# The tanh rows of an additive-attention kernel in a ring of 10240 columns in place of eight buffers, with half the descriptor scratch

## Chip, cores and metric

The program runs on one core of a Trainium2 chip. The metric is the device time of one execution in microseconds (us); the time before is the median of three runs. The profile is one execution of the same program, recorded instruction by instruction.

## The reference, cut to what matters

Eight images of 56x56 positions with 128 channels go through two layers. The first is a deformable convolution with an MLP. The second is causal additive attention over the S = 3136 positions of an image, then an expert layer that picks eight tokens for each of 64 experts. The change touches the attention scores alone:

```python
f = jnp.einsum('bih,ha->bia', x, W1[:h])
g = jnp.einsum('bjh,ha->bja', x, W1[h:])
t = jnp.tanh(f[:, :, None, :] + g[:, None, :, :] + b1)
scores = jnp.einsum('bija,a->bij', t, w2[:, 0]) + b2[0]
e = jnp.exp(scores) * flag
```

For each pair of a query i and an earlier key j there are A = 16 tanh values, which are weighted and summed to one score.

## The kernel before, in words

**Blocks, chunks, units, groups.** The positions of an image are cut into NBLK = 25 blocks of 128 queries (the last has 64). Block k attends to the key tiles 0 to k. `chunks_of(k)` cuts these k + 1 tiles into the fewest equal chunks of at most CHUNK = 1024 keys, so a chunk is 128 to 1024 columns wide. A *unit* is one ScalarE instruction: the tanh of eight queries times 16 values (128 partitions) against the keys of a chunk (`what == "unit"`, L1678). A full chunk has 16 units, and PLACES = 4 *groups* of four units (two in the last block). TensorE reduces a group with `score_w` into a bank pair of PSUM (`what == "score"`, L1846); `score_ps` holds two chunks. When all four groups of a chunk are scored, ScalarE takes the exponential (`what == "exp"`, L1688), and TensorE and VectorE turn it and multiply it with the values. An image has 800 units, 208 groups and 52 chunks.

**The tanh buffers.** `tanh` is `[128, TANH_SLOTS, CHUNK]`, eight buffers of 1024 columns. Unit `ui` writes the first w columns of buffer `ui % 8`. Before that it waits on the semaphore `scored` until the group of unit `ui - 8` has been scored.

**The other work.** The same engines run the convolution (`image_in`, `conv`, `offsets`, `weights`), the chain of each block (`turn`, `mix`, `hidden`, `mlp_out`, `keys`) and the sampling. For the sampling GpSimd (POOL) issues the gathers: one `sample` step is SAMPLES = 18 indirect DMAs (L1189), each fetching 128 rows of 512 bytes into one of GATHER_SLOTS = 4 buffers. VectorE multiplies and sums a buffer (L1373, L1376), and that frees it: POOL waits on `sampled` for it. There are NSUB = 49 sample steps for an image, 392 in all, and two of them feed a block's chain, whose end (`keys`, L1418 to L1421) the first unit of the block waits for (`keys_copied`).

**The order of work.** Each engine runs its steps in one fixed order, with no choice at run time. The order comes from a planner in the kernel: `needs()` lists what each step waits for, `due_times()` gives priorities and `simulate()` lays the steps out by the costs in `LASTS` and `lasts()`. The period so found is repeated for each image by a loop (`walk`); the first and last images have orders of their own. In the order that the planner gives for the kernel before, ScalarE has its `exp` of a chunk 0 to 4 units behind the last unit of the chunk in 44 of the 52 chunks, and between 6 and 24 units behind in the other eight. In that plan POOL is busy without a pause, and the wait for the tanh buffers is what starts 23 of the 800 units.

**After the last image**, parts of `tanh` hold the last image's routing scores (`tanh_flat`, `score7`, `chosen7`, `chosenT7`), 8064 columns in all.

**Descriptor scratch.** The program is built with the default of 16384 bytes per partition, kept for the descriptors of the DMAs that POOL issues.

Of the kernel before, what the change touches and what calls it, by code (L numbers as in the profile page):

```python
# [8 lines left out]
ACT = mybir.ActivationFunctionType  # L9
# [3 lines left out]
P = 128  # L13
# [18 lines left out]
CHUNK = 1024  # L32
# [4 lines left out]
GATHER_SLOTS = 4  # L37
PIECE = 3
X1_SLOTS = 10
TANH_SLOTS = 8  # L40
PLACES = 4
FLOOR_MAGIC = 8388608.0
RSQRT_MAGIC = 1597463007.0 - 2.0 ** 30 - 2.0 ** 22
# [10 lines left out]
def chunks_of(k):  # L54

    tiles = k + 1
    n = -(-tiles * P // CHUNK)
    cuts = [tiles * i // n for i in range(n + 1)]
    return [list(range(cuts[i], cuts[i + 1])) for i in range(n)]


def chunk_width(tiles):
    return sum(blk_rows(j) for j in tiles)
# [77 lines left out]
def group_of(k, c, s):  # L141

    return k, c, s // (blk_rows(k) // 32)


UNIT_GROUP = [GROUP_INDEX[group_of(*u)] for u in UNIT_INDEX]


SLOT_OF = [0, 1, 2, 3] * 10 + [0, 1, 2] * 3
# [127 lines left out]
def needs():  # L277
# [3 lines left out]
    def at(age, engine, what, *place):  # L281
        return age, engine, (what, *place)
# [64 lines left out]
        out["sp", ("logits", k)] = [at(0, "dve", "logits", k), at(0, "sp", "route", k)]  # L347
    for i, u in enumerate(units):
        ci = CHUNK_INDEX[u[:2]]
        ring = units[i - TANH_SLOTS if i >= TANH_SLOTS or UNITS % TANH_SLOTS == 0 else -1]  # L350
        out["act", ("unit", *u)] = [at(0, "dve", "keys", u[0]), at(int(i < TANH_SLOTS), "pe", "score", *group_of(*ring))]
        if u[2] == group_units(u[0], group_of(*u)[2])[-1]:
            out["pe", ("score", *group_of(*u))] = [at(0, "act", "unit", *u),
                                                   at(int(ci < 2), "act", "exp", *chunks[ci - 2])]
# [335 lines left out]
def network(nc, io, x2_d, xln2_d, logits_d, patches_d, chosen_d, expert_d, out, images):  # L690
    with ExitStack() as ctx:
        def sb(name, shape, dt=F32):
            return ctx.enter_context(nc.sbuf_tensor(name, shape, dt))
# [4 lines left out]
        def sem(name):  # L698
# [64 lines left out]
        key_rep = sb("key_rep", [P, EARLY * P + S])  # L763
        query = sb("query", [P, NBLK * A])
        values = sb("values", [P, NBLK + EARLY, C + 1])
        tanh = sb("tanh", [P, TANH_SLOTS, CHUNK])
        expo = sb("expo", [P, 2, CHUNK])
        expoT = sb("expoT", [P, 2, 4, P])
        den = sb("den", [P, 2])
# [33 lines left out]

        slots = [pool_mem[:, at:at + 2 * PER * HID].rearrange("p (w e h) -> p w e h", w=2, e=PER)
                 for at in SLOTS_AT]
        tanh_flat = tanh[:].rearrange("p a b -> p (a b)")
        score7 = tanh_flat[:E, 0:S]
        chosen7 = tanh_flat[:E, S:2 * S]
        chosenT7 = tanh_flat[:ROW_P, 2 * S:2 * S + ROW_T * E].rearrange("p (t e) -> p t e", e=E)
# [830 lines left out]
        @block.scalar  # L1640
        def _(act):
            for ln in (h_ready, mask_exp, gelu_done, tanh_done, exp_done):
                nc.scalar.sem_inc(ln.sem, ln.lead)
            act.wait_ge(consts_ready, 1)

            def wait(ln, image, i):
                act.wait_ge(ln.sem, ln.after(image, i))

            def task(n, odd, name):
                what, i = (*name, 0)[:2]  # L1650
                if what == "conv":
                    wait(conv_done, n, i)
                    wait(params_done, n, i - 1)
                    nc.scalar.activation(h_band[:], side_ps[:, :BAND], ACT.Gelu, bias=bn[:, 1:2], scale=bn[:, 0:1])\
                        .then_inc(h_ready.sem, 1)
                elif what == "offsets":
                    wait(mask_shifted, n, i)
                    nc.scalar.activation(mask[:], mask[:], ACT.Exp).then_inc(mask_exp.sem, 1)
                elif what == "hidden":
                    r = blk_rows(i)  # L1660
                    wait(hid_done, n, i)
                    wait(mlp_done, n, i - 1)
                    for c in range(HID // P):
                        last = nc.scalar.activation(hid[:, c, :r], chain_ps[:, c * P:c * P + r], ACT.Gelu,  # L1664
                                                    bias=b_hid[:, c:c + 1])
                    last.then_inc(gelu_done.sem, 1)
                elif what == "unit":
                    k, c, s = name[1:]
                    ui = UNIT_INDEX[k, c, s]
                    if (c, s) == (0, 0):  # L1670
                        wait(keys_copied, n, k)

                    wait(scored, n, UNIT_GROUP[ui - TANH_SLOTS] - (GROUPS_SCORED if ui < TANH_SLOTS else 0))
                    tiles = chunks_of(k)[c]
                    w = chunk_width(tiles)
                    lo = key_column(odd, tiles[-1] if odd else tiles[0])
                    col = k * A + row_group(k, s)
                    nc.scalar.activation(tanh[:, ui % TANH_SLOTS, :w], key_rep[:, lo:lo + w], ACT.Tanh,  # L1678
                                         bias=query[:, col:col + 1]).then_inc(tanh_done.sem, 1)
                elif what == "exp":  # L1680
                    k, c = name[1:]
                    r = blk_rows(k)
                    ci = CHUNK_INDEX[k, c]
                    w = chunk_width(chunks_of(k)[c])
                    wait(scored, n, GROUP_INDEX[k, c, PLACES - 1])

                    wait(exp_turned, n, last_quad_of_chunk(ci - 2))
                    nc.scalar.activation(expo[:r, ci % 2, :w], score_ps[:r, ci % 2, :w], ACT.Exp, bias=tiny[:r, 2:3])\  # L1688
                        .then_inc(exp_done.sem, 1)

                elif what == "u_exp":
                    r = E * len(units[i])
                    act.wait_ge(differ_ready, i + 1)
                    nc.scalar.activation(score[:r], score[:r], ACT.Exp, bias=neg[:r], accum_out=total[:r, 0:1])
                    nc.scalar.drain().then_inc(prob_ready, 1)
                elif what == "e_gelu":
                    act.wait_ge(e_biased, STEPS)
                    nc.scalar.activation(pre, pre, ACT.Gelu).then_inc(e_act, 1)
                elif what == "l_exp":
                    act.wait_ge(last_top, 1)  # L1700
                    nc.scalar.activation(score7, score7, ACT.Exp, bias=neg[:E], accum_out=total[:E, 0:1])
                    nc.scalar.drain().then_inc(last_prob, 1)
                elif what == "l_gelu":
                    act.wait_ge(last_biased, i + 1)
                    part = pre7[:, :, i * PER:(i + 1) * PER]
                    nc.scalar.activation(part, part, ACT.Gelu).then_inc(last_act, 1)

            walk(act, "act", task)

        @block.tensor  # L1710
        def _(pe):
# [10 lines left out]
            def wait(ln, image, i):  # L1722
                pe.wait_ge(ln.sem, ln.after(image, i))
# [25 lines left out]
            def task(n, odd, name):  # L1749
# [84 lines left out]
                elif what == "score":  # L1834
# [8 lines left out]
                    for lo in range(0, w, 512):  # L1843
                        hi = min(w, lo + 512)
                        for col, ui in enumerate(four):
                            last = mm(score_ps[32 * col:32 * col + 32, ci % 2, lo:hi], score_w[:, place],  # L1846
                                      tanh[:, ui % TANH_SLOTS, lo:hi], start=place == 0, stop=place == PLACES - 1)
                    last.then_inc(scored.sem, 1)
                elif what == "values":
                    k, c, q = name[1:]  # L1850
# [277 lines left out]
```

## Time and profile before

| | us |
|---|---|
| median of 3 runs | 15138.87 |
| lowest, highest | 15132.04, 15160.17 |
| profiled execution | 15154.41 |
| its span, first to last instruction | 15152.6 |
| ScalarE busy | 6766.0 (45%) |
| TensorE matmul busy | 7392.2 (49%) |
| VectorE busy | 6055.5 (40%) |
| POOL busy | 6690.9 (44%) |

A row of a view names the engine, the source line, the operation and its tiles (out<-in), and the idle time before it in square brackets with what ended it. The start of a matmul in the profile is when TensorE takes it up, and its end is modelled. "remote" as what ended a wait means that the semaphore rose at a time at which no instruction was seen to end.

### The profile page before, as it was taken

The page shows a single profiled execution, that of the slowest core. Times are in us where ns is not written, and L with a number is a line of the kernel's source. Part 1 is how long each engine was busy: PE and PEld are TensorE (multiplying, and loading weights), DVE is VectorE, ACT ScalarE, POOL GpSimd, SP SyncE. Part 2 cuts the span into 40 slices and gives each one's busy share as a digit, 9 for nine tenths or more (in the row PEclk, how much of TensorE's full clock was granted, in tenths as well). Part 3 has the DMA queues.
Part 4 walks back from the last instruction along what each step waited for, and adds up shares of the span by engine and source line. Part 5 has one row for each costly group of instructions (what it writes and reads, how often), then busy time and mean ns, then how long its engine had stood idle before and what let it go on. Part 6 is the DMA issues. An engine that isn't in the chain of part 4 may idle for free.

```text
span 15152.6 us, 152058 instructions
## 1 busy us (share of the span) xinstructions
PE 7392.2 (49%) x45113; PEld 3712.8 (25%) x45113; DVE 6055.5 (40%) x17780; ACT 6766.0 (45%) x8210; POOL 6690.9 (44%) x7060
## 2 busy tenths in 40 slices
PE   3345553445534555345444455444554445544557
PEld 1222222222222222122222222222222222222234
DVE  4443334433443334344344433434334434354343
ACT  1245642455424554245533455334553346533454
POOL 4444444444444444444444444444444444444430
PEclk6667776677766777677766677667776677766778
DMA  2111111111111111111111111111111111212325
GB/s 63 52 44 35 34 40 48 43 32 35 42 46 41 32 38 43 45 40 32 39 41 45 39 33 39 42 47 38 33 37 43 48 37 32 58 55 70 95 63 161
DMA packets 453936, 712.02 MB, mean 47 GB/s; under 512 B 146576, under 2 KB 261136, under 8 KB 451472
## 3 DMA queue, kind: packets, MB, share of 16 engines
q0 software_dynamic: 225792, 462.87, 11.6%
q1 hardware_dynamic: 227312, 239.24, 5.0%
q8 instruction: 378, 6.19, 0.2%
q14 instruction: 454, 3.72, 0.1%
HBM read 595.58 MB, written 105.96 MB: 46 GB/s over the span
## 4 chain that ended last, share of the span: by engine, by line
another core or an unknown queue 37%; ACT 20%; PE 13%; issue 12%; DVE 12%; DVEq 5%; DMA 1%; SPq 0%; POOL 0%; ACTq 0%; POOLq 0%
ACT tanh L1678 17%; PE score_ps L1846 6%; DVEq L1208 4%; DVE pool_mem L1373 2%; DVE newton L1242 2%; PE value_ps L1875 2%; DVE rstd L1244 1%; PE side_ps L1778 1%; DVE bst L1249 1%; ACT L1664 1%; PE turn_ps L1747 1%; ACT expo L1688 1%; ACT L1688 1%; ACT hid L1664 1%
## 5 line engine op out<-in xcount | busy, mean ns | idle before, releaser
L1678 ACT ACTIVATE tanh<-key_rep,query 128x896 f32<-128x896 f32 (+7 forms) x6400 | 5557.8, 951 | 5014.7 <-remote 2819.6
L1189 POOL DMA_INDIRECT pool_mem<-patches_odd,pool_mem x3528 | 3346.8, 949 | 4037.8 <-DVE y L1376 3014.6
L1189 POOL DMA_INDIRECT pool_mem<-patches_even,pool_mem x3528 | 3344.0, 948 | 3988.4 <-DVE y L1376 2890.2
L1846 PE MATMUL score_ps<-tanh,score_w 128*32 128x512 f32 (+3 forms) x24320 | 3613.8, 639 | 2235.8 <-ACT tanh L1678 1285.3
L1846 PEld LDWEIGHTS score_ps<-tanh,score_w 128*32 128x32 f32 x24320 | 832.7, 125 | 4411.0 <-issue 2787.7
L1875 PE MATMUL value_ps<-values,expoT 128*128 128x129 f32 (+1 forms) x5200 | 1009.8, 345 | 341.9 <-issue 275.8
L1373 DVE TENSOR_TENSOR pool_mem<-pool_mem 128x384 f32<-128x384 f32 x2352 | 1135.8, 552 | 50.7 <-issue 49.1
L1376 DVE TENSOR_REDUCE y<-pool_mem 128x64 f32<-128x2304 f32 x392 | 1000.8, 2553 | 53.2 <-issue 24.7
L1875 PEld LDWEIGHTS value_ps<-values,expoT 128*128 128x128 f32 (+1 forms) x5200 | 891.6, 248 | 435.4 <-issue 350.3
L1747 PE MATMUL turn_ps<-ident,expo 128*128 128x128 f32 (+1 forms) x2632 | 564.1, 339 | 830.6 <-DVE expoT L1442 433.6
L1442 DVE COPY expoT<-turn_ps 128x512 f32<-128x512 f32 (+4 forms) x800 | 457.1, 572 | 1203.2 <-remote 843.6
L1688 ACT ACTIVATE expo<-score_ps,tiny 128x896 f32<-128x896 f32 (+9 forms) x416 | 383.1, 921 | 831.9 <-remote 666.9
L1688 ACT ACT_TABLE_LOAD x206 | 264.3, 1283 | 883.9 <-remote 697.6
L1747 PEld LDWEIGHTS turn_ps<-ident,expo 128*128 128x128 f32 (+1 forms) x2632 | 381.9, 175 | 1000.1 <-DVE expoT L1442 458.1
L1266 DVE TENSOR_TENSOR biased<-chain_ps,rows 128x128 f32<-128x128 f32 (+1 forms) x400 | 115.3, 288 | 1234.4 <-remote 880.4
L1242 DVE SCALAR_TENSOR_TENSOR newton<-rstd,newton 128x1 f32<-128x1 f32 (+1 forms) x2403 | 529.1, 220 | 193.0 <-issue 14.3
L1815 PE MATMUL chain_ps<-chainT,w_fc 128*128 128x128 f32 (+1 forms) x1600 | 328.0, 371 | 512.3 <-DVE chainT L1395 412.4
L1664 ACT ACTIVATE hid<-chain_ps,b_hid 128x128 f32<-128x128 f32 (+1 forms) x800 | 226.3, 365 | 709.8 <-remote 504.0
L1822 PE MATMUL chain_ps<-w_fc,hid 128*128 128x128 f32 (+1 forms) x1600 | 281.8, 330 | 421.2 <-ACT hid L1664 288.3
L1831 PE MATMUL chain_ps<-chainT,w_key 128*128 128x128 f32 (+1 forms) x400 | 142.6, 457 | 704.6 <-DVE chainT L1411 505.4
L1244 DVE SCALAR_TENSOR_TENSOR rstd<-newton,rstd 128x1 f32<-128x1 f32 (+1 forms) x2403 | 385.1, 160 | 213.3 <-issue 21.9
L1778 PE MATMUL side_ps<-pool_mem,early 128*128 128x448 f32 x1008 | 423.3, 575 | 93.2 <-DVEq L1208 87.5
(166 smaller groups left out, 6210.9 us busy)
## 6 DMA issues: line engine op xcount, KB each, us to landing
pool_mem<-in_weight SPq DMA_DIRECT2D x64, 1024.0 KB, 9.2
pool_mem<-patches_even,pool_mem POOLq DMA_INDIRECT x3528
pool_mem<-patches_odd,pool_mem POOLq DMA_INDIRECT x3528
patches_even<-pool_mem SPq DMA_DIRECT2D x104, 256.0 KB, 2.0
patches_odd<-pool_mem SPq DMA_DIRECT2D x104, 256.0 KB
pool_mem<-in_x SPq DMA_DIRECT2D x56, 224.0 KB
x_tok<-in_x SPq DMA_DIRECT2D x192, 64.0 KB
x_d<-x SPq DMA_DIRECT2D x192, 64.0 KB
```

The source lines that it names most:

```text
L1189: pool.indirect_dma_start(gathered[:, b, j * 4 * CG:(j + 1) * 4 * CG], None, patches_flat[int(odd)], bass.IndirectOffsetOnAxis(ap=index[:, ...
L1208: return v.drain()
L1242: v.scalar_tensor_tensor(newton[:r, 1:2], rstd[:r], rstd[:r], newton[:r, 0:1], ALU.mult, ALU.mult)
L1244: v.scalar_tensor_tensor(rstd[:r], newton[:r, 1:2], 1.5, rstd[:r], ALU.add, ALU.mult)
L1373: v.tensor_tensor(part, part, weight[:, lo:lo + PIECE].unsqueeze(2) .to_broadcast([P, PIECE, CG, 4]), ALU.mult)
L1376: v.tensor_reduce(y[:, i // 2 % 2, b].rearrange("p (g c) -> p g c", c=CG), product.rearrange("p (g t) c k -> p g c t k", g=2), AX_XY, ALU. ...
L1678: nc.scalar.activation(tanh[:, ui % TANH_SLOTS, :w], key_rep[:, lo:lo + w], ACT.Tanh, bias=query[:, col:col + 1]).then_inc(tanh_done.sem, 1)
L1688: nc.scalar.activation(expo[:r, ci % 2, :w], score_ps[:r, ci % 2, :w], ACT.Exp, bias=tiny[:r, 2:3])\
L1747: return mm(out, src, ident[:r, :r], is_transpose=True, start=True, stop=True)
L1778: last = mm(side_ps[:, :BAND], taps[:, t], x_pad[:, i * BAND_ROWS + dy:(i + 1) * BAND_ROWS + dy, dx:dx + W], start=t == 0, stop=t == TAPS - 1)
L1846: last = mm(score_ps[32 * col:32 * col + 32, ci % 2, lo:hi], score_w[:, place], tanh[:, ui % TANH_SLOTS, lo:hi], start=place == 0, stop=pl ...
L1875: last = mm(value_ps[:r, :C + 1], expoT[:wj, pi % 2, z, :r], values[:wj, value_place(odd, j)], start=j == 0, stop=j == k)
```

## The change

The rows of `tanh` are packed: a unit gets w columns of a ring of TANH_COLUMNS = 10240, directly behind the unit before it, or at column 0 where it does not fit before the end. `tanh_before(i)` finds the latest earlier unit whose columns overlap those of unit i, and the wait is for that unit's group. The same rule goes to the planner's `needs()`, so the order of the engines may change. The descriptor scratch is halved to 8192 bytes per partition; the ring takes the 2048 more columns of four bytes that this leaves.

```diff
-TANH_SLOTS = 8
+TANH_COLUMNS = 10240
+def tanh_ring():
+    places, at = [], 0
+    for k, c, s in UNIT_INDEX:
+        w = chunk_width(chunks_of(k)[c])
+        at = 0 if at + w > TANH_COLUMNS else at
+        places.append((at, at + w))
+        at += w
+    return places
+TANH_AT = tanh_ring()
+def tanh_before(i):
+    lo, hi = TANH_AT[i]
+    for j in range(i - 1, i - UNITS - 1, -1):
+        a, b = TANH_AT[j % UNITS]
+        if a < hi and lo < b:
+            return j
+TANH_BEFORE = [tanh_before(i) for i in range(UNITS)]
...
-        ring = units[i - TANH_SLOTS if i >= TANH_SLOTS or UNITS % TANH_SLOTS == 0 else -1]
-        out["act", ("unit", *u)] = [at(0, "dve", "keys", u[0]), at(int(i < TANH_SLOTS), "pe", "score", *group_of(*ring))]
+        ring = TANH_BEFORE[i]
+        out["act", ("unit", *u)] = [at(0, "dve", "keys", u[0]), at(int(ring < 0), "pe", "score", *group_of(*units[ring]))]
...
-        tanh = sb("tanh", [P, TANH_SLOTS, CHUNK])
+        tanh = sb("tanh", [P, TANH_COLUMNS])
...
-                    wait(scored, n, UNIT_GROUP[ui - TANH_SLOTS] - (GROUPS_SCORED if ui < TANH_SLOTS else 0))
+                    old = TANH_BEFORE[ui]
+                    wait(scored, n, UNIT_GROUP[old] - (GROUPS_SCORED if old < 0 else 0))
...
-                    nc.scalar.activation(tanh[:, ui % TANH_SLOTS, :w], key_rep[:, lo:lo + w], ACT.Tanh,
+                    nc.scalar.activation(tanh[:, TANH_AT[ui][0]:TANH_AT[ui][1]], key_rep[:, lo:lo + w], ACT.Tanh,
...
-                                      tanh[:, ui % TANH_SLOTS, lo:hi], start=place == 0, stop=place == PLACES - 1)
+                                      tanh[:, TANH_AT[ui][0] + lo:TANH_AT[ui][0] + hi], start=place == 0, stop=place == PLACES - 1)
...
-    nc = bacc.Bacc("TRN2", target_bir_lowering=False, num_devices=1)
+    nc = bacc.Bacc("TRN2", target_bir_lowering=False, num_devices=1, dynamic_dma_scratch_size=8192)
```

## Rows read from the trace of the kernel before

**Rows 1.** The page: span, busy time, and the chain that ended last.
```profile
span 15152.6 us, 152058 instructions
PE 7392.2 (49%) x45113; PEld 3712.8 (25%) x45113; DVE 6055.5 (40%) x17780; ACT 6766.0 (45%) x8210; POOL 6690.9 (44%) x7060
...
another core or an unknown queue 37%; ACT 20%; PE 13%; issue 12%; DVE 12%; DVEq 5%; DMA 1%; SPq 0%; POOL 0%; ACTq 0%; POOLq 0%
ACT tanh L1678 17%; PE score_ps L1846 6%; DVEq L1208 4%; DVE pool_mem L1373 2%; DVE newton L1242 2%; PE value_ps L1875 2%; DVE rstd L1244 1%; PE side_ps L1778 1%; DVE bst L1249 1%; ACT L1664 1%; PE turn_ps L1747 1%; ACT expo L1688 1%; ACT L1688 1%; ACT hid L1664 1%
```

**Rows 2.** Busy time in stretches: without gathers, then with them, then inside one burst.
```profile
core 0: us, PE busy (x) PEld busy (x) DVE busy (x) ACT busy (x) POOL busy (x), PEclk, DMA share, GB/s
14720.00:14935.00 215.00, 185.35 (x1296) 101.38 (x1297) 93.45 (x285) 211.12 (x223) 0.00 (x0) 0.93 0.30 92
3000.00:4000.00 1000.00, 519.28 (x3214) 242.65 (x3215) 379.59 (x1114) 546.54 (x615) 448.13 (x474) 0.74 0.14 36
...
2067.70:2084.00 16.30, 7.25 (x14) 1.16 (x13) 3.12 (x14) 0.00 (x0) 10.89 (x12) 0.75 0.25 69
```

**Rows 3.** Timeline of POOL: first two and last gather of one burst.
```profile
2059.73 0.94 POOL L1189 DMA_INDIRECT pool_mem<-patches_odd,pool_mem  x1 [24.04 <-DVE y L1376]
2060.98 0.95 POOL L1189 DMA_INDIRECT pool_mem<-patches_odd,pool_mem  x1 [0.30 <-issue]
...
2080.99 0.94 POOL L1189 DMA_INDIRECT pool_mem<-patches_odd,pool_mem  x1 [0.30 <-issue]
```

**Rows 4.** Timeline of PE over the same burst.
```profile
2064.33 1.92 PE L1846 MATMUL score_ps<-tanh,score_w 128*32 128x512 f32 x16
...
2071.79 0.61 PE L1846 MATMUL score_ps<-tanh,score_w 128*32 128x512 f32 x1 [0.81 <-issue]
2073.88 0.59 PE L1846 MATMUL score_ps<-tanh,score_w 128*32 128x512 f32 x1 [1.49 <-issue]
2076.01 1.01 PE L1846 MATMUL score_ps<-tanh,score_w 128*32 128x512 f32 x1 [1.54 <-issue]
2078.82 1.01 PE L1846 MATMUL score_ps<-tanh,score_w 128*32 128x512 f32 x1 [1.80 <-issue]
```

**Rows 5.** Timeline of ACT over the same burst, and over another.
```profile
2060.96 4.26 ACT L1678 ACTIVATE tanh<-key_rep,query 128x1024 f32<-128x1024 f32 x4
2085.16 5.31 ACT L1678 ACTIVATE tanh<-key_rep,query 128x1024 f32<-128x1024 f32 x5 [19.94 <-remote]
...
3012.89 7.57 ACT L1678 ACTIVATE tanh<-key_rep,query 128x896 f32<-128x896 f32 x8 [12.18 <-DVEq L1208]
3038.14 8.50 ACT L1678 ACTIVATE tanh<-key_rep,query 128x896 f32<-128x896 f32 x9 [17.69 <-remote]
```

**Rows 6.** Waits of ACT: us in total, times, longest us.
```profile
ACT tanh L1678 <- remote: 2819.6, 249, 43.7
ACT tanh L1678 <- DVEq L1208: 1104.0, 82, 29.5
ACT tanh L1678 <- PE score_ps L1846: 730.3, 165, 26.7
ACT L1688 <- remote: 697.6, 56, 36.5
ACT expo L1688 <- remote: 666.9, 61, 21.9
```

**Rows 7.** The tanh line: duration ns min/median/max, and a sample of its shapes.
```profile
L1678 ACT ACTIVATE tanh<-key_rep,query x6400: 384/943/1167, 285.4 to 14947.5; 128x896 f32<-128x896 f32 x56, 128x768 f32<-128x768 f32 x55, 128x1024 f32<-128x1024 f32 x38, 128x640 f32<-128x640 f32 x23
```

**Rows 8.** Groups by line: the tanh units and the scores.
```profile
L1678 ACT ACTIVATE tanh<-key_rep,query 128x896 f32<-128x896 f32 (+7 forms) x6400 | 5557.8, 951 | 5014.7 <-remote 2819.6
L1846 PE MATMUL score_ps<-tanh,score_w 128*32 128x512 f32 (+3 forms) x24320 | 3613.8, 639 | 2235.8 <-ACT tanh L1678 1285.3
```

**Rows 9.** Waits of POOL, and of DVE.
```profile
POOL pool_mem L1189 <- DVE y L1376: 5904.7, 349, 37.5
POOL pool_mem L1189 <- issue: 2048.9, 6706, 2.3
...
DVE biased L1266 <- remote: 880.4, 89, 31.9
DVE chainT L1411 <- remote: 858.2, 77, 18.8
```

**Rows 10.** DMA issues: KB each, median us from issue to landing.
```profile
patches_even<-pool_mem SPq DMA_DIRECT2D x104, 256.0 KB, 2.0
```

More of the change, by code:

```diff
@@ L805, in network @@
                  for at in SLOTS_AT]
-        tanh_flat = tanh[:].rearrange("p a b -> p (a b)")
+        tanh_flat = tanh[:]
         score7 = tanh_flat[:E, 0:S]
```

## Prediction

> **What bounds the kernel now.** The page comes first. No engine is busy for half of the span, and the chain that ended last holds 37% of "another core or an unknown queue", with ACT tanh at 17% and the scores at 6% [rows 1]. One core runs here, so those 37% are semaphores that rose long after the instruction that should have raised them. The next view is the windows. In the stretch after the last gather ACT is busy for 211.12 of 215 us; between 3000 and 4000 us, with gathers, for 546.54 of 1000 [rows 2]. So something goes with the gathers, and the timelines of one burst show what.
>
> POOL begins a burst of 18 gathers at 2059.73 and one gather follows another every 1.25 us until 2081.93 [rows 3]. PE still takes up 16 score matmuls in 1.92 us at 2064.33; from 2071.79 on it takes up one in 2.1 to 2.8 us, waiting for nothing that the profile shows [rows 4]. ACT finishes four tanh units and stands still from 2065.22 until 2085.16, 3.2 us after the burst's end [rows 5]. In the 16.3 us from 2067.7 ACT does nothing at all [rows 2]. Around 3012 it is the same: ACT does eight units, exactly the eight buffers, and stands for 17.69 us [rows 5]. I read it so: in the later part of a burst PE gets almost nothing finished, its queue fills with matmuls that it has taken up but not done, and their semaphores come when the burst is over. There are 392 bursts. With 15152.6 us that is one in 38.7 us, of which the burst is 22.2 us and POOL's wait for VectorE most of the rest (5904.7 us in 349 waits, 16.9 us each) [rows 1, 3, 9].
>
> Why PE slows, I can't tell from this trace, and I assume that the change doesn't touch it. What the change does touch is how far ACT gets while PE is held up.
>
> **The ring.** Two kinds of wait can be shortened by it: tanh units that wait for "remote" (2819.6 us, 249 times) and for the scores (730.3 us, 165 times), together 3549.9 us in 414 waits, 8.6 us each [rows 6]. Not shortened are the waits for the keys (1104.0 us) and those of the exponential (697.6 + 666.9 us) [rows 6], which need all scores of their chunk.
>
> How many more units fit: I worked out from `tanh_ring` and `tanh_before` how far back each unit's blocker lies. Before it is 8 units for all. After it is on average 9.9 units for chunks of 1024 columns, 11.0 for 896, 12.9 for 768 and 15.7 for 640, and for none of the 800 is it fewer than 9. The tanh line's sample of shapes has 38, 56, 55 and 23 of these widths [rows 7], so the mean gain is (38 x 1.9 + 56 x 3.0 + 55 x 4.9 + 23 x 7.7) / 172 = 4.0 units. A wait is for a group of four either way, so there is no loss by rounding: the first unit of a group is the one that stops, and it is followed by as many as the ring is longer.
>
> What ends the gain early is the exponential. It stands in ACT's order mostly 0 to 4 units behind a chunk's 16 units and can't be passed. A wait for a buffer can stand 1 to 11 units ahead of it; spread evenly, the smaller of that and 4 is (1 + 2 + 3 + 8 x 4) / 11 = 3.45 units. A unit costs 5557.8 / 6400 = 0.87 us [rows 8], so 3.0 us for each wait, and 414 x 3.0 = 1240 us. Some of the waits are shorter than that (the 165 for scores are 4.4 us on average), and some are at a block's first unit, which waits for its keys as well. I take off a fifth: about 1000 us of tanh work moves under waits that are there anyway.
>
> **What of it the span gets back.** Below: ACT tanh is 17 of the 63 points of the chain that are not "unknown" [rows 1], which gives 27% of the 1000, 270 us. Above: in the stretch without gathers ACT is the bound at 98% [rows 2], which gives 980 us. The true share lies between, since after a burst VectorE, PE and ACT all have work piled up: PE is 49% busy, VectorE 40%, ACT 45% [rows 1]. I take 40%, nearer to the chain, because the chain is of the whole span and the gather-free stretch is 215 us of it: 400 us. PE's extra backlog at a burst's end doesn't eat it: it takes 16 score matmuls of a group in 1.92 us [rows 4], and ACT needs 4.26 us for the four units [rows 5]. At half the clock that would be near 3.8 us, still less.
>
> **The planner.** The rule goes into `needs()`, so orders can change. In the plan of before the buffers start only 23 of 800 units, and POOL is its bound, so I expect few steps to move, and these a few units of 0.87 us [rows 8]. Bounds: 23 units in each of 8 images, each 0.87 us early or late, are 160 us both ways. I take 0, since a unit that moves ahead of an exponential pushes back that one and pulls up itself.
>
> **The instruction edits.** Each unit still has one wait, one activation and one increment, and each score matmul the same shape; the addresses differ. Both kinds of row stay at their durations; 0 us. That the tail's use of `tanh` now begins inside a ring costs nothing, since it waits for the last exponential as before.
>
> **The halved scratch.** POOL waits 0.31 us between two gathers, 2048.9 us in 6706 times [rows 9], and 0.30 us at the second and at the last gather of a burst alike [rows 3]: a lack of room for descriptors does not show now. Below, the cost is 0. Above, POOL would have to wait once in each burst for one transfer to land; the nearest row is a store of patches with 2.0 us to landing [rows 10], so 392 x 2.0 = 784 us, and the burst holds PE for as much longer. I take 0, since the gap does not grow along a burst and POOL then pauses for 16.9 us on average.
>
> [...] No row here shows descriptors.
>
> **The sum.** 15154.4 us of the profiled execution (span 15152.6) - 400 = 14754. The median of the runs is 15.5 us under the profiled one, so 14740 us.
>
> **Rivals.**
> - *The ring gives, and ACT was the bound* (980 us back): 14160. For it speaks the gather-free stretch [rows 2]; against it that the chain has more "unknown" than ACT [rows 1].
> - *The time hangs on the bursts and on VectorE, not on ACT.* VectorE's own waits for late semaphores (880.4 us, 858.2 us in its two largest) [rows 9] decide when a sample is taken, and so when the next burst begins. ACT then does its units earlier and waits longer at the exponential and at `hidden`. The gain is 0 to 30 us: 15110 to 15140. For it speaks that the exponential's waits are already 1364.5 us [rows 6].
> - *The scratch is too small, slower.* Place: L1189 on POOL. Price: 2.0 us a burst [rows 10], 784 - 400 = 384 us more than before, 15520. It decides from 400 / 392 = 1.0 us a burst on. Against it: POOL's even gaps [rows 3, 9]. For it: nothing in the trace, but the mechanism that holds PE goes with the bursts, and what sets its length is unknown.
> - *The change doesn't do what it says*: chunks of 1024 gain only two units, and half of the waits could be there. Then 414 x 2 x 0.87 x 0.4 = 290 us at most, still faster; it is within the first case.
>
> **How the numbers follow.** Within 0.2% (30 us) a measurement of this kernel can hardly tell from no change. Chances: my forecast with its own range of 14400 to 15050, 0.57; ACT the bound, under 14400, 0.10; hanging on the bursts, 0.19, of which 0.13 within 30 us, 0.04 faster and 0.02 slower; scratch or another loss that goes with the bursts, 0.14, of which 0.13 slower and 0.01 the same. Faster 0.57 + 0.10 + 0.04 = 0.71, same 0.14, slower 0.15. The range runs from 14330 to 15180: it leaves out most of the second case and nearly all of the fourth, about 2 in 10.
>
> **What the profile after would show.** ACT tanh waits for remote and scores at 2400 to 2700 us in place of 3550, with runs of 10 to 16 units where eight stood; the exponential's waits longer, 1400 to 1900 us; POOL's gap still 0.30 us and its burst 22.2 us; POOL's wait for DVE y down by some 400 us, to 5500. The busy times stay within 1%. Wrong would be: a POOL gap over 0.31 us, a longer stand of PE behind a burst's end than 3.2 us, or tanh waits that shrink while the exponential's grow by as much.

## The result, and the profile after

| | before | after |
|---|---|---|
| median of 4 runs, us | 15143.46 | 14941.74 |
| lowest, highest | 15132.04, 15160.17 | 14916.75, 14982.08 |
| profiled execution | 15154.41 | 14929.51 |
| its span | 15152.6 | 14927.7 |

The ratio is 0.9873, with a 95% interval of 0.9852 to 0.9893 (the quotient of the two medians, 0.9867, lies in it), and the medians are 202 us apart. The forecast was 14740 us, 403 us under before. The kernel became faster, as forecast, by half of what was forecast. All line numbers after `tanh_before` are 26 or 27 higher in the kernel after.

The page of the kernel after: span, busy time, the chain, the tanh units and the scores. It answers to [rows 1, 8].

```profile
span 14927.7 us, 152204 instructions
PE 7337.2 (49%) x45113; PEld 3721.1 (25%) x45113; DVE 6039.6 (40%) x17780; ACT 6781.7 (45%) x8224; POOL 6699.7 (45%) x7060
...
another core or an unknown queue 33%; issue 17%; DVE 15%; PE 15%; ACT 13%; DVEq 6%; DMA 1%; SPq 0%; POOL 0%; ACTq 0%; POOLq 0%
...
L1705 ACT ACTIVATE tanh<-key_rep,query 128x896 f32<-128x896 f32 (+7 forms) x6400 | 5546.6, 951 | 3892.6 <-remote 1325.4
```

The work is the same to within 1% on each engine. What moved is idle time: 5014.7 us ahead of the tanh units before [rows 8], 3892.6 us now. In the chain ACT fell from 20 to 13 points and the unknown part from 37 to 33; issue, DVE and PE rose by 5, 3 and 2.

Waits of ACT in the kernel after (us in total, times, longest us), beside [rows 6]:

```profile
ACT tanh L1705 <- remote: 1325.4, 158, 44.2
ACT tanh L1705 <- PE score_ps L1873: 949.7, 166, 41.7
ACT expo L1715 <- remote: 821.5, 69, 37.3
ACT tanh L1705 <- issue: 811.5, 59, 22.9
ACT tanh L1705 <- DVEq L1234: 805.3, 67, 38.7
ACT L1715 <- remote: 730.0, 49, 28.1
ACT expo L1715 <- PE score_ps L1873: 390.5, 82, 35.8
ACT hid L1690 <- PE chain_ps L1842: 387.2, 57, 24.1
```

The tanh waits for remote and scores are 1325.4 + 949.7 = 2275.1 us, 1275 less than the 3549.9 of before. A part of that is a change of name: the tanh's idle time put down to issue rose from 360.0 to 811.5 us, and that for the keys fell from 1104.0 to 805.3. All idle time ahead of the tanh units fell by 1122 us (5014.7 to 3892.6). The exponential's waits (L1715, its table load with it) are up, from 1711.3 to 2476.8 us over all rows.

POOL's waits in the kernel after, beside [rows 9]:

```profile
POOL pool_mem L1215 <- DVE y L1402: 5668.1, 342, 48.4
POOL pool_mem L1215 <- issue: 2055.1, 6713, 2.6
```

The gap between two gathers is 2055.1 / 6713 = 0.306 us, as before. POOL waits 237 us less for VectorE. Its last gather starts at 14493.9 us, where before it started at 14716.4, so 222.5 of the 225 us are won by the end of the gathers. This is bookkeeping and names no cause: POOL's issuing (POOL busy 6690.9 us before, 6699.7 after) and its gaps (2048.9 and 2055.1 us in all) kept their length, so its waits must shrink with the time to its last gather, whichever engine set the pace.

One burst after, first POOL (first two gathers, last), then ACT, then PE. This burst ends at 3056.61.

```profile
3034.45 0.94 POOL L1215 DMA_INDIRECT pool_mem<-patches_odd,pool_mem  x1 [11.13 <-DVE y L1402]
3035.70 0.94 POOL L1215 DMA_INDIRECT pool_mem<-patches_odd,pool_mem  x1 [0.30 <-issue]
...
3055.67 0.94 POOL L1215 DMA_INDIRECT pool_mem<-patches_odd,pool_mem  x1 [0.30 <-issue]
```

```profile
3034.06 13.36 ACT L1705 ACTIVATE tanh<-key_rep,query 128x896 f32<-128x896 f32 x14
3059.50 1.15 ACT L1705 ACTIVATE tanh<-key_rep,query 128x1024 f32<-128x1024 f32 x1 [12.09 <-remote]
3061.04 1.01 ACT L1715 ACTIVATE expo<-score_ps,tiny 128x896 f32<-128x896 f32 x1 [0.39 <-PE score_ps L1873]
```

```profile
3051.69 0.80 PE L1873 MATMUL score_ps<-tanh,score_w 128*32 128x384 f32 x1 [1.51 <-issue]
3053.80 0.80 PE L1873 MATMUL score_ps<-tanh,score_w 128*32 128x384 f32 x1 [1.32 <-issue]
3056.59 0.80 PE L1873 MATMUL score_ps<-tanh,score_w 128*32 128x384 f32 x1 [1.99 <-issue]
3058.69 2.23 PE L1873 MATMUL score_ps<-tanh,score_w 128*32 128x384 f32 x5 [1.30 <-issue]
```

PE is held as in [rows 4], one matmul in 2.1 to 2.8 us. ACT now does 14 units in a row where it did 8 in a burst before [rows 5] and stands for 12.09 us where it stood 17.69, until 2.9 us after the burst.

The last image, by a window from the end of the last tanh unit to the end of the span (14948.5 to 15152.6 us before), before and after:

```profile
14948.50:15152.60 204.10, 129.42 (x1089) 92.67 (x1085) 61.81 (x117) 8.68 (x20) 0.00 (x0) 0.67 0.65 207
```

```profile
14705.40:14927.70 222.30, 144.36 (x1159) 102.38 (x1155) 65.66 (x123) 9.58 (x21) 0.00 (x0) 0.67 0.63 201
```

So the profiled difference of 225 us is 243 won up to the last tanh unit, and 18 given back behind it, with 70 matmuls more there. Whether those 18 us are a loss is taken up under **The last image**.

### The profile page after: what moved, and what is told of

The parts are those of the page before. It is cut to its first block, busy times and chain, and to the rows that moved or that the text cites. A ratio compares the mean times of both kernels' runs of the same rounds, so it can differ in the third digit from the quotient of the medians.

```text
span 14927.7 us, 152204 instructions
## 1 busy us (share of the span) xinstructions
PE 7337.2 (49%) x45113; PEld 3721.1 (25%) x45113; DVE 6039.6 (40%) x17780; ACT 6781.7 (45%) x8224; POOL 6699.7 (45%) x7060
## 4 chain that ended last, share of the span: by engine, by line
another core or an unknown queue 33%; issue 17%; DVE 15%; PE 15%; ACT 13%; DVEq 6%; DMA 1%; SPq 0%; POOL 0%; ACTq 0%; POOLq 0%
ACT tanh L1705 11%; PE score_ps L1873 7%; DVEq L1234 6%; DVE pool_mem L1399 3%; DVE newton L1268 2%; PE value_ps L1902 2%; DVE rstd L1270 2%; PE side_ps L1805 1%; PE turn_ps L1774 1%; DVE bst L1275 1%; PE chain_ps L1842 1%; DVE expoT L1468 1%; DVE y L1402 1%; DVE mv L1277 1%
## 5 line engine op out<-in xcount | busy, mean ns | idle before, releaser
L1705 ACT ACTIVATE tanh<-key_rep,query 128x896 f32<-128x896 f32 (+7 forms) x6400 | 5546.6, 951 | 3892.6 <-remote 1325.4
L1873 PE MATMUL score_ps<-tanh,score_w 128*32 128x512 f32 (+3 forms) x24320 | 3560.0, 636 | 1786.5 <-ACT tanh L1705 851.2
L1873 PEld LDWEIGHTS score_ps<-tanh,score_w 128*32 128x32 f32 x24320 | 865.3, 125 | 3903.8 <-issue 2779.9
L1715 ACT ACTIVATE expo<-score_ps,tiny 128x896 f32<-128x896 f32 (+9 forms) x416 | 384.3, 924 | 1545.4 <-remote 821.5
L1842 PEld LDWEIGHTS chain_ps<-chainT,w_fc 128*128 128x128 f32 x1600 | 295.2, 276 | 729.7 <-DVE chainT L1421 571.9
L1774 PE MATMUL chain_ps<-ident,values 128*128 128x128 f32 (+1 forms) x200 | 79.0, 395 | 782.9 <-DVE values L1431 424.2
```

What stands on the lines that cost most here:

```text
L1705: nc.scalar.activation(tanh[:, TANH_AT[ui][0]:TANH_AT[ui][1]], key_rep[:, lo:lo + w], ACT.Tanh, bias=query[:, col:col + 1]).then_inc(tanh_ ...
L1774: return mm(out, src, ident[:r, :r], is_transpose=True, start=True, stop=True)
L1842: last = mm(chain_ps[:, c * P:c * P + r], w_fc1[:, c * P:(c + 1) * P], chainT[:, :r], start=True, stop=True)
```

## Experiments

**Two levels of chips.** The kernel before took about 15140 us in the first measurement and on two chips later, and about 9427 us on three others. No chip was seen at both levels; why a chip is at one of them stays open. Each kernel is therefore told with the time of the kernel before on the same chip. The two levels have different bounds (of the chain of the kernel after POOL has 0% on a held chip and 65% on a free one; see the last section too), and a verdict of one says nothing of the other. "Held" chips are those of 15140 us, "free" ones those of 9427 us.

| kernel | held: median, ratio [interval] | free: median, ratio [interval] |
|---|---|---|
| after | 14941.74, 0.9873 [0.9852, 0.9893] | 9441.34, 1.0016 [1.0007, 1.0025] |
| ring, order of before | 14909.04, 0.9846 [0.9828, 0.9865] | 9423.82, 0.9996 [0.9987, 1.0005]; 9420.99, 0.9993 [0.9984, 1.0002]; 9421.79, 0.9997 [0.9988, 1.0007] |
| after, last image ordered as before | 14945.46, 0.9867 [0.9848, 0.9887] | 9422.65, 0.9999 [0.9989, 1.0008] |
| before, scratch halved | 15129.89, 1.0001 [0.9991, 1.001] | 9427.54, 0.9998 [0.9989, 1.0007] |
| packed ring of 8192 columns | 15154.38, 1.0013 [1.0003, 1.0023] | 9428.24, 1.0001 [0.9992, 1.001] |
| after, exponential due later | 14900.62, 0.9852 [0.9831, 0.9873] | 9444.24, 1.0019 [1.001, 1.0028]; 9443.83, 1.0017 [1.0008, 1.0026] |

**The kernel after on a free chip.**

> The changed kernel once more. In the first four runs of experiments the kernel before took 9426.59 us, not 15143, with PE taking up matmuls at full pace inside the bursts, so the two measurements stand for two conditions of the chip. If this call falls in the condition of the first measurement: about 14940 us against 15143 us. If it falls in the other: POOL's bursts are the bound (64% of the chain), ACT has slack, and the change gives nothing: 9420 to 9450 us against 9427 us.

It is 15 us slower there. The chain of that run, and POOL's waits:

```profile
POOL 65%; issue 22%; ACT 5%; DVE 3%; PE 2%; DMA 2%; DVEq 1%; SPq 0%; POOLq 0%; ACTq 0%
```

```profile
POOL pool_mem L1215 <- issue: 2144.9, 7038, 0.3
POOL pool_mem L1215 <- DVEq L1234: 70.8, 1, 70.8
POOL pool_mem L1215 <- DVE y L1402: 5.2, 17, 0.3
```

POOL issues gathers without a pause and hardly ever waits for VectorE (5.2 us, against 5668.1). While POOL issues without a pause, a change that only frees ACT earlier can take from POOL at most these 5.2 us. What remains of the change is a loss, and the next two experiments place it in the order of the last image.

**Ring or order of steps.** The ring stays, but the planner is told of eight buffers, so each engine has the order of before:

```diff
-        ring = TANH_BEFORE[i]
+        ring = i - 8
```

> The changed kernel, but the planner is still told of eight buffers, so every engine keeps the order of before; the ring is there at run time alone. Theory A (ring waits move to the exponential): the ring is felt at run time, so most of the gain stays: 14900 to 15000 us, tanh waits for remote and scores under 2600 us in place of 3550. Theory B (the gain of 202 us came from the planner's new order): 15110 to 15160 us. Theory C (the ring gave the 400 us that I forecast and the new order cost half of it): about 14740 us.

> The ring at run time with the order of before. In the condition of the first measurement, theory A (felt at run time): 14900 to 15000 us; theory B (the gain is the planner's new order): 15110 to 15160 us; theory C (the order cost half of the ring's 400 us): about 14740 us. In the other condition: within 20 us of before, as e1 was.

> The ring at run time with the order of before, a third time, for the case that this call falls in the condition of the first measurement: theory A (felt at run time) 14880 to 15000 us, theory B (new order of the loop) 15110 to 15160 us. In the other condition 9416 to 9428 us, as twice before.

> The ring of the change with the order that the planner makes for eight buffers. If the kernel before takes about 15140 us on this chip, as in the first measurement: the theory that the loop's gain comes from the ring at run time expects the ratio at 0.987 or below (the ring's part of -243 us and no part of the +18 us behind the last tanh); the theory that the planner's new order brought the gain expects 0.998 to 1.002. If the kernel before takes about 9427 us here, both expect what was measured under that condition already, 0.9993 to 0.9997.

On the held chip it is 0.9846, 236 us under before: the gain is the ring's at run time. The new order brings nothing. The interval overlaps that of the kernel after, measured elsewhere; the fairer comparison is with the next experiment, which ran on the same held chip and differs only in the order of the loop. It took 14945.46 us at the median against 14909.04 here, and all four executions of the one lie above all four of the other (14934.85 and up, 14918.05 and down). By this one pair the new order of the loop costs 36 us there. On the free chips it costs nothing (9422.65 against 9421.79 us on one chip), and the loss of the kernel after is gone. The other half, the new order with eight buffers, was not tried: its steps would wait for each other in a circle.

**The last image.** Only `last_order` is made by the rule of eight buffers:

```diff
-    due, need = {**due_times(), **late_due}, {**needs(), **late}
+    due, need = {**due_times(), **late_due}, {**needs(True), **late}
```

> The changed kernel, with the order of the last image planned by the rule of eight buffers; the ring is there at run time and in the order of all other images. In the changed kernel's plan 28 of the 49 c_mix steps stand behind the last score step in PE's order, in the kernel before and in this one 23. Theory E (the order of the last image costs 18 us, from 204 to 222 us between the last tanh and the end): 9416 to 9428 us where the changed kernel took 9441.34, or about 14922 us in the condition of the first measurement. Rival (the loop's order or the addresses cost it): 9436 to 9446 us.

> The kernel after with only the last image's order made as for eight buffers. If the kernel before takes about 15140 us here: 18 us under the kernel after, ratio 0.986. If it takes about 9427 us: 0.9999 as measured, since nothing but the tail differs.

On the free chip 19 us come back. On the held one they don't: the median is 14945.46, where 18 us less than 14941.74 were expected. The window from the end of the last tanh unit is shorter, as expected:

```profile
14751.10:14954.30 203.20, 133.78 (x1089) 93.54 (x1085) 61.85 (x117) 8.72 (x21) 0.00 (x0) 0.65 0.65 208
```

203 us and 1089 matmuls, as before. But the window ahead of it, from the last gather to the end of the last tanh unit, is longer. First the kernel after, then this run:

```profile
14493.90:14705.40 211.50, 179.34 (x1246) 94.29 (x1245) 86.37 (x261) 206.83 (x220) 0.94 (x1) 0.92 0.30 89
```

```profile
14512.40:14751.10 238.70, 209.74 (x1439) 109.35 (x1440) 96.16 (x291) 227.72 (x242) 0.95 (x1) 0.92 0.30 89
```

The kernel after has 27 us and 193 matmuls less there, and 19 us more behind. From the last gather to the end it takes 433.8 us, this run 441.9 us, the ring with the order of before 443.1 us, and the kernel before 436.2 us. So on a held chip the order of the last image moves work behind the last tanh unit, and no loss is left. On the free chips the same stretch is 388.9 us in the kernel after and 377.0 us here: there 12 us of loss are left. Up to the last gather this run took 18.5 us longer than the kernel after, with the same order of the loop; single executions of the kernel after differ by more (14916.75 to 14982.08). In TensorE's order of the last image 28 of the 49 steps named `c_mix`, of 14 matmuls each, stand after the last score in the kernel after, 23 before: 5 x 14 = 70 matmuls, the ones counted behind the last tanh unit.

**The scratch alone.** The kernel before, with one edit:

```diff
-    nc = bacc.Bacc("TRN2", target_bir_lowering=False, num_devices=1)
+    nc = bacc.Bacc("TRN2", target_bir_lowering=False, num_devices=1, dynamic_dma_scratch_size=8192)
```

> The kernel before with the descriptor scratch halved and nothing else. Theories A and B: no difference, 15110 to 15175 us, POOL's gap between gathers still 0.30 us. Theory D (the halved scratch cost the half of the 400 us that is missing): about 15340 us, with a longer burst or a longer stand of PE behind it.

> The kernel before with half the descriptor scratch and nothing else. Under the condition in which the kernel before takes 15143 us the theory that the ring carries the whole gain expects 0.998 to 1.002; the theory that the smaller scratch changed the bursts expects a ratio of 0.985 to 0.992, and the POOL gap of 0.306 us between two gathers changed. Under the 9427 us condition: 0.9998, as measured.

Nothing at either level: 1.0001 and 0.9998.

**The ring in the bytes of the eight buffers.** The kernel after, its own order made for the smaller ring, with the default scratch:

```diff
-TANH_COLUMNS = 10240
+TANH_COLUMNS = 8192
```

> The packed ring in the 8192 columns of before with the default scratch; the planner is told of it. The blocker then lies 8 units back for 1024 columns, 9 for 896, 10 for 768, 12 for 640. Theory A: packing gives a part of the gain, 15000 to 15090 us, with tanh waits between those of the two kernels. Theory D: 14850 us or less, since the scratch is whole. Theory B: anything within 100 us of 14940, going with the order and not with the size.

> The ring packed by width in 8192 columns, the bytes of the eight buffers, with the default scratch. If the time goes with the tanh tiles that fit (about 8 x 1024/730 = 11 units here, 14 in the ring of 10240), about half of the gain is kept under the 15143 us condition: ratio 0.990 to 0.994; if three units more are enough, all of it: 0.985; if nothing is gained below 14 units, 1.000. Under the 9427 us condition: 1.0001, as measured.

No gain, 1.0013. Waits of ACT:

```profile
ACT tanh L1705 <- remote: 2768.4, 221, 39.4
...
ACT tanh L1705 <- PE score_ps L1873: 701.8, 180, 22.0
```

The blocker of a unit, the earlier unit whose columns it needs, lies 9.9 units back on average here, 12.5 in the ring of 10240 and 8 before (units at the start of an image, whose blocker is in the image before, left out). The two units more took 80 us from the tanh waits (3470.2 from 3549.9), the next 2.6 units 1195 us. A wait is for the blocker's whole group of four. Worked out from `TANH_BEFORE` and `UNIT_GROUP`, this ring lets only 338 of the 800 units wait for an earlier group than the eight buffers do, and 12 wait for a later one; in the ring of 10240 it is 652, and none waits for a later one. That fits a gain that comes late. Whether it is the reason, or this ring's own order, these runs can't tell: the ring of 8192 with the order of before was not run.

**The exponential later.** If ACT stops at an exponential that stands too early, moving it back lets tanh units pass:

```diff
-            due["exp", k, c] = end
+            due["exp", k, c] = end + 8 * d
```

In the plan the exponential then stands 8.9 units behind its chunk's last unit on average (3.7 before, 5.9 after).

> The changed kernel with the exponential due eight units later in the planner, so that it stands 8 or more units behind its chunk's last unit in all chunks of the wider blocks, in place of mostly 1 to 4. Theory A (the exponential in ACT's order is the barrier that took over the ring's waits): the exponential's waits fall from 2476 us to under 1500, and 100 to 250 us more come back, 14700 to 14840 us. Rival (the time hangs on the gather bursts and VectorE): the waits fall and the time stays within 60 us of 14940, or rises, as values and finish come later.

> The changed kernel with the exponential eight units later in the order. In the condition of the first measurement, theory A (the exponential in ACT's order took over the ring's waits): 14700 to 14840 us and its waits under 1500 us; rival (bursts and VectorE set the time): within 60 us of 14940, or slower. In the other condition: 9435 to 9450 us, as e5 was.

> The kernel after with the exponential's due time made eight score steps later still (its step stood 5.88 units behind its chunk's last unit on average in the kernel after, 3.65 before). If the exponential's early place is what ate the gain under the 15143 us condition, the ratio falls below that of the kernel after (0.987) by 0.003 or more and the exponential's waits by 300 us or more; if the time hangs on PE, which hands out scores and turned rows late whatever stands first on ACT, it stays at 0.987 or rises. Under the 9427 us condition: 1.0018, as measured.

Waits of ACT on the held chip:

```profile
ACT tanh L1705 <- remote: 2274.1, 214, 42.0
...
ACT tanh L1705 <- PE score_ps L1873: 771.7, 153, 41.9
ACT hid L1690 <- PE chain_ps L1842: 671.0, 70, 24.1
...
ACT expo L1715 <- remote: 416.7, 36, 20.4
...
ACT L1715 <- remote: 296.5, 17, 26.9
```

All waits of ACT by what stands at its head, summed over the rows of the waits view of each profiled execution, in us:

| waits at | before | after | ring, old order | ring of 8192 | exponential late |
|---|---|---|---|---|---|
| tanh, for remote or scores | 3549.9 | 2275.1 | 1847.6 | 3470.2 | 3045.8 |
| tanh, for the keys, or issue | 1464.0 | 1616.8 | 1641.5 | 1439.4 | 1658.5 |
| exponential | 1711.3 | 2476.8 | 2417.0 | 2138.9 | 1277.8 |
| hidden | 786.7 | 907.7 | 1129.8 | 400.9 | 1185.5 |
| rest | 816.7 | 792.5 | 1066.2 | 894.0 | 873.8 |
| all | 8328.6 | 8068.9 | 8102.1 | 8343.4 | 8041.4 |
| span | 15152.6 | 14927.7 | 14908.5 | 15148.5 | 14884.7 |

The later exponential took 1199 us from its own waits, and the tanh units and `hidden` took 771 + 278 of them. The sum moved by 27 us. The median is 41 us under the kernel after, with overlapping intervals and on another chip: the ratio fell by 0.0021, between the 0.003 that would have spoken for the exponential as the barrier and the 0 that would have spoken against it. On the free chips it takes what the kernel after takes.

**Holding PE on a free chip.** On a free chip the hold was imitated: at 45 places of a middle image PE waits, 6 us behind a sample step of the plan, until the burst that this sample step makes room for has landed. The computation is the whole one.

```diff
+                for pos, (age, step) in enumerate(order_of(name, schedule)):
+                    for a, t in held.get(pos, []) if name == "pe" else []:
+                        slot, each = gather_slot(t), 16 * SAMPLES
+                        engine.wait_ge(gather_done[slot], (n - a) * (SLOT_USES[slot] * each) + (slot_use(t) + 1) * each)
```

> The kernel before with 45 more waits for each of the middle six images: at the PE step that stands 6 us behind a sample step in the plan, PE waits until the gather burst that this sample sets free has landed. So PE is held in the later part of most bursts, as it was in the first measurement, on a chip that does not do it by itself. Expected if bursts then follow samples as there (22.4 us of burst and some 10 to 16 us between): 12500 to 15500 us, ACT tanh waiting for remote, scores or DMA-held PE for over 2000 us. If the holds are mostly over when PE comes to them: under 10500 us, and the three that follow tell little.

> The changed kernel with the same holds. Theory A: faster than the held kernel before by 0.7 to 2.5%, with the tanh waits down by a third and the exponential's waits up by more than half of that. Rival (bursts and VectorE alone set the time): within 0.3%.

> The ring at run time with the order of before, with the same holds. Theory A (felt at run time): at least half of the gain of the changed held kernel. Theory B (the new order made it): within 0.3% of the held kernel before. Theory C (the new order costs): faster than the changed held kernel.

> The changed kernel with the exponential eight units later and the same holds. Theory A (the exponential in ACT's order is the barrier behind the ring): its waits fall to under half, and the time is 0.5 to 2% under that of the changed held kernel. Rival: the waits fall and the time stays within 0.3% or rises.

Medians: before held 13592.28, after held 13573.23, ring with the old order held 13569.23, exponential late held 13627.64 (ratios to the unheld kernel before on that chip, 9424.48: 1.442, 1.4399, 1.4394, 1.4456). Waits of ACT, before held and then after held:

```profile
ACT tanh L1704 <- PE score_ps L1872: 2103.4, 254, 24.6
...
ACT hid L1690 <- PE chain_ps L1841: 973.3, 61, 37.2
ACT L1714 <- PE score_ps L1872: 561.0, 90, 20.4
ACT expo L1714 <- PE score_ps L1872: 271.7, 72, 21.2
```

```profile
ACT hid L1716 <- PE chain_ps L1868: 1303.9, 95, 31.7
ACT tanh L1731 <- PE score_ps L1899: 1032.6, 113, 23.6
ACT expo L1741 <- PE score_ps L1899: 563.3, 74, 21.0
ACT expo L1741 <- PE turn_ps L1800: 507.1, 36, 29.7
```

The ring takes 1071 us from the tanh waits for scores and gives 19 us, far from the 0.7% expected if the ring's waits were the limit and inside the 0.3% of its rival. Most of the rest turns up at the exponential (953.7 to 1531.3 us over all its rows) and at `hidden` (1224.7 to 1531.6), as on the held chip. The exponential moved later costs 54 us here. The imitation isn't the real hold: there the same ring gives 202 us.

## Why the prediction was wrong, point by point

- **The reading of a burst: right.** PE is still held in the later part of a burst, with one matmul in 2.1 to 2.8 us before and after, and ACT stops when its room is full: for 17.69 us behind eight units before [rows 4, 5], for 12.09 us behind 14 units after.
- **The ring: right, and more than forecast.** About 1000 us of tanh work was to move under the waits; the waits for remote and scores fell by 1275, and by 1702 with the old order (all idle time ahead of the tanh units by 1122 and 1525). They were forecast at 2400 to 2700 us and are 2275. The 4.0 units more of room came from a sample without the narrow chunks; over all 800 units the blocker lies 13.3 units back, 5.3 more than before. And there is some rounding: 148 of the 800 units wait for the same group as before.
- **What of it the span gets back: the step that failed.** I took 40% of 1000 us, with 27% of it as the lower bound: 400 us. The ring with the old order, which tests this term alone, gave 236 us by the medians, so some 164 of the missing 201 us are here (it ran on another held chip). In shares: 243 of 1275 us up to the last tanh unit, 19%, and with the old order 244 of 1702 (last tanh unit at 14704.1), 14%. The bound was unsound: ACT's share of the chain says where the chain ran, not how much of a wait is returned when the next step on ACT waits too. The ledger shows the taker: the exponential +766 us and `hidden` +121 for tanh's -1275. Both need scores and products from PE, and most of the exponential's waits end with "remote", as the tanh's did; that it is the same hold of PE is read from this and not tested by itself. It is the mechanism of the rival in which the time hangs on the bursts and on VectorE; its price, 0 to 30 us, was too low for held chips. Moving the exponential shows the same from the other side: 1199 us of its waits went elsewhere, and the span kept 43 at most. So neither kind of ACT wait comes back to the span in full, and what does come back is a small part.
- **What sets the pace in place of ACT** was not isolated. POOL's waits for VectorE fell by 237 us, forecast 400, and the last gather came 222.5 us sooner, but as said that follows from any faster loop. That the ring gives 236 us where POOL waits 5904.7 us for VectorE, and next to nothing (3 to 6 us by the medians) on free chips, where the ring with the old order has 6.7 to 7.6 us of such waits in three profiled executions, fits a pace set by the moment at which POOL gets a free gather buffer. Which steps made VectorE earlier stays open.
- **The planner: 0 was taken, and "few steps move" was wrong.** The exponentials' places in the loop moved (3.7 to 5.9 units behind the chunk's last unit on average), and the pair on one held chip puts the price of the new order at 36 us, inside the bounds of 160. That is the rest of the missing 201 us as far as medians of four tell. The order of the last image moved 18 us behind the last tanh unit and took 27 us from ahead of it: no loss on a held chip, 12 to 19 us on a free one.
- **The halved scratch: 0, right.** The scratch alone gave 1.0001 on a held chip and 0.9998 on a free one, and POOL's gap between two gathers stayed at 0.305 us there (2047.2 us in 6707 times, and 2143.0 in 7032), where the kernel before has 0.306. The 0 was an estimate from that gap. No run shows the descriptors themselves, so how near the halved scratch is to being full stays open.
- **The instruction edits: 0, right.** Tanh units take 951 ns at the mean before and after.
- **What the profile was to show.** The exponential's two waits for remote are 821.5 + 730.0 = 1551.5 us (forecast 1400 to 1900), ACT's stand behind a burst 2.9 us (3.2 before), busy times within 1%. The sign named as fatal, tanh waits that shrink while the exponential's grow by as much, came to 766 of 1275: it was there in good part.

The profiled executions: 15154.4 - 243 + 18 = 14929 us. The 243 and the 18 are cut from the same two spans at the last tanh unit, so this sum closes by itself and proves nothing.

## What to carry to other kernels

Before a removed wait is priced, ask what the next instruction on that engine waits for: if that one waits too, most of the wait moves one step on (here 81%). An engine's share of the chain is no lower bound for what a cut wait gives back (here 27% by the chain, 19% measured). And a planner that is told of more room changes orders elsewhere, so the room and the order are worth separate runs: here the room gave 236 us and the order cost part of it. Time lost behind one mark, as the last tanh unit, is a loss only if it wasn't won ahead of it.

## What the runs showed of the hardware

**The same kernel at 15140 and at 9427 us.** The kernel before took 15144.83 and 15134.68 us at the median on two chips and 9426.59 (9424.48 later), 9426.69 and 9426.97 on three. The program is the same, POOL issues a gather in 0.944 us at the median with a gap of 0.30 at both levels, and the DMA queue of the gathers is busy for 11.6% of 15152.6 us = 1758 us on a held chip and, in the kernel before with the scratch halved, 10.7% of 15166.1 us = 1623 us on another held chip and 18.1% of 9428.9 us = 1707 us on a free one. What differs is TensorE in the later part of a burst. Two stretches with 10 gathers each, the kernel after on a held chip and then on a free one (busy us and instructions of PE, its loads, DVE, ACT and POOL, then the granted clock):

```profile
3012.00:3024.50 12.50, 0.45 (x2) 0.45 (x3) 0.29 (x1) 1.78 (x2) 8.58 (x10) 0.57 0.20 52
```

```profile
3018.00:3030.00 12.00, 6.79 (x55) 3.44 (x55) 8.03 (x20) 11.94 (x16) 9.26 (x10) 1.00 0.22 62
```

PE takes up 2 matmuls on the one and 55 on the other. The granted clock was 0.57 in the first and 1.00 in the second, and a factor of 1.75 in the clock doesn't make one of 27 in the matmuls. In the stretch on the free chip the 10 gathers don't hold PE, which takes up 55 matmuls beside them in 12 us. What holds PE on the held chips beside the same gathers, no run here shows.

**In between.** One of the 21 executions of the kernel before on the last free chip took 10992.95 us. So a chip left its level for one execution; what did it is not known.
